# A recommendation tower on one core: eleven one-hot tables instead of ten, three one-hot slots instead of two, and gathers that are waited for by pairs of groups

## The reference

```python
e = jnp.stack([tbl_0[ids[:, 0]], ..., tbl_25[ids[:, 25]]], axis=1)
combined = jnp.concatenate([e, r_dense_x[:, None, :]], axis=1)     # (2048, 27, 128)
interact = jnp.einsum('bfd,bgd->bfg', combined, combined)
z = interact[:, TRIU_I, TRIU_J]                                    # 351 pairs
h = jnp.concatenate([z, r_dense_x], axis=1)
h = jnp.maximum(h @ W_top1 + b_top1, 0.0)                          # 479 x 512
h = jnp.maximum(h @ W_top2 + b_top2, 0.0)                          # 512 x 256
y = h @ W_top3                                                     # 256 x 1
```

## Time and profile before

| | us |
|---|---|
| median of 3 runs (lowest 556.6, highest 562.27) | 556.9 |
| the profiled execution: its time | 551.39 |
| its span, first to last instruction | 549.5 |
| PE busy / DVE / ACT / POOL | 476.3 / 315.8 / 233.9 / 248.9 |
| instructions | 9188 |

### The profile page before, as it was taken

How to read it: one execution, slowest core, us unless ns; L and a number is a source line. 1 busy time by engine, 2 the same in 40 slices (tenths; PEclk the granted TensorE clock), 3 DMA queues, 4 the chain that set the end, 5 groups by cost and what they waited for, 6 DMA issues and landing times.

```text
span 549.5 us, 9188 instructions
## 1 busy us (share of the span) xinstructions
PE 476.3 (87%) x3544; PEld 436.3 (79%) x3544; DVE 315.8 (57%) x503; ACT 233.9 (43%) x755; POOL 248.9 (45%) x266
## 2 busy tenths in 40 slices
PE   3786677998888998899898998989998898899988
PEld 3676576897887888789788888879897887889977
DVE  6994137564467535675366654775367543676252
ACT  3532225443444343534435344443545335354454
POOL 6435554455555554455545445554554545420000
PEclk9998569899899998999999999999999899999999
DMA  8551111111111111111111111111111101100000
GB/s 291 189 151 40 37 38 34 39 39 48 35 39 35 44 39 35 39 38 44 35 35 38 35 49 40 39 35 43 35 40 35 39 24 40 35 21 0 1 2 1
DMA packets 12511, 25.80 MB, mean 47 GB/s; under 512 B 4931, under 2 KB 6603, under 8 KB 12458
## 3 DMA queue, kind: packets, MB, share of 16 engines
q0 software_dynamic: 8192, 16.79, 11.5%
q1 hardware_dynamic: 4276, 8.42, 4.8%
HBM read 25.18 MB, written 0.01 MB: 46 GB/s over the span
## 4 chain that ended last, share of the span: by engine, by line
PE 71%; DVE 10%; DMA 6%; POOL 5%; issue 5%; ACT 2%; another core or an unknown queue 1%; POOLq 0%; DVEq 0%; ACTq 0%
PE x_ps L437 23%; PE gram_ps L453 23%; PE tail_ps L508 13%; DVE onehot L617 8%; DMA raw<-in_tbl,ids_sb 6%; POOL raw L398 4%; PE x_ps L415 4%; PE ids_ps L423 3%; PE tail_ps L478 2%; DVE gram L279 2%; PE tail_ps L487 2%; PE tail_ps L514 2%; DVE split_weights L638 1%; ACT xt L552 0%
## 5 line engine op out<-in xcount | busy, mean ns | idle before, releaser
L398 POOL DMA_INDIRECT raw<-in_tbl,ids_sb x256 | 245.6, 959 | 234.7 <-DMA raw<-in_tbl,ids_sb 161.4
L617 DVE TENSOR_TENSOR onehot<-ids_ps,row_no 128x1024 fp32r<-128x1024 f32 (+1 forms) x160 | 206.7, 1303 | 77.3 <-PE x_ps L437 50.1
L437 PE MATMUL x_ps<-onehot,hot_hi 128*128 128x256 f32 x688 | 185.0, 302 | 24.3 <-DVE onehot L617 17.7
L437 PE MATMUL x_ps<-onehot,hot_lo 128*128 128x256 f32 x688 | 174.4, 286 | 0.0
L437 PEld LDWEIGHTS x_ps<-onehot,hot_hi 128*128 128x128 f32 x688 | 133.3, 194 | 33.2 <-issue 16.4
L453 PE MATMUL gram_ps<-xt 128*128 128x108 f32 x1024 | 137.6, 289 | 14.1 <-DVE gram L279 11.2
L453 PEld LDWEIGHTS gram_ps<-xt 128*128 128x128 f32 x1024 | 129.7, 203 | 21.6 <-ACT gram L279 13.9
L279 DVE COPY gram<-gram_ps 32x104 f32<-32x104 f32 x256 | 68.6, 268 | 117.1 <-PE gram_ps L453 99.7
L437 PEld LDWEIGHTS x_ps<-onehot,hot_lo 128*128 128x128 f32 x688 | 133.6, 194 | 0.0
L279 ACT COPY gram<-gram_ps 32x104 f32<-32x104 f32 x256 | 60.4, 236 | 103.0 <-PE gram_ps L453 73.3
L552 ACT COPY xt<-x_ps 128x256 f32<-128x256 f32 x80 | 49.7, 621 | 99.7 <-PE x_ps L437 91.4
(11 more groups left out here) (48 smaller groups left out, 267.9 us busy)
## 6 DMA issues: line engine op xcount, KB each, us to landing
raw<-in_tbl,ids_sb POOLq DMA_INDIRECT x256, 2.5
table_home<-in_tbl SPq DMA_DIRECT2D x4, 512.0 KB, 8.8
table_home<-in_tbl SPq DMA_DIRECT2D x2, 640.0 KB, 4.2
raw<-in_tbl SPq DMA_DIRECT2D x2, 512.0 KB, 4.7
dense_sb<-in_dense_t SPq DMA_DIRECT2D x8, 128.0 KB
gram<-in_tbl SPq DMA_DIRECT2D x1, 640.0 KB, 12.2
h<-in_tbl SPq DMA_DIRECT2D x1, 512.0 KB, 11.2
h<-in_w SPq DMA_DIRECT2D x1, 256.0 KB
```

What stands on the lines that cost most here:

```text
L398: nc.gpsimd.indirect_dma_start(out=raw[k][:, f, :], out_offset=None, in_=tables[f], in_offset=bass.IndirectOffsetOnAxis(ap=ids_sb[:, t, f: ...
L437: last = nc.tensor.matmul(ps, table[:, chunk_at[j] + c, :], onehot[:, p % RING, c - a, :], start=(c == 0 and table is hot_hi), stop=(c == ...
L617: nc.vector.tensor_tensor(onehot[:, p % RING, 0:n, :], ids_ps[:, it % 2, :].unsqueeze(1).to_broadcast([P, n, BLOCK]), row_no[chunks[it % n ...
```

## The change

- `HOT` 10 to 11: one table of 1250 rows (10 chunks) becomes an item of each block; 15 tables are gathered, in groups of 4, 4, 4 and 3.
- `RING` 2 to 3.
- POOL waits for landed gathers only before groups 0 and 2 of a tile, and there for both of the groups before.
- Room for this in SBUF: `DENSE` 3 to 2; the hot ids are loaded block by block (2 slots, 128 partitions, cleared by POOL first, 11 rows filled by SP) and rounded by DVE block by block; `pick`, 1280 values on 10 partitions, becomes a rounded identity whose column is broadcast as the weights of the ids matmul; `zt` in whole is gone: DVE subtracts `zt_hi` straight from PSUM and gives the bank back; `table_home` reaches over more of the later tiles, so that nine tables load without waiting; the second half of w2 is loaded only after the first part of w1 is split.
- Tail steps are stretched over the 18 pieces of the hot phase and 3 positions more, `TAIL_OVER`, and those past the last piece go between the grams of the first tile.

```diff
-HOT = 10
+HOT = 11
-DENSE = 3
-RING = 2
+DENSE = 2
+RING = 3
-SPREAD = 1.2
+TAIL_OVER = 3
...
-        scale = SPREAD * n / tail_at[-1] if tail_of else 0
+        scale = (n + TAIL_OVER) / tail_at[-1] if tail_of else 0
+        left = [(at * scale, step) for step, at in zip(tail_of, tail_at)]
...
         for i in range(n):
-            steps += [step for step, at in zip(tail_of, tail_at) if i - 1 < at * scale <= i]
+            while left and left[0][0] <= i:
+                steps.append(left.pop(0)[1])
             steps += hot_steps(first + i, first + i + 1)
             steps += [turn for turn, at in zip(turns[0], turn_at) if at == i]
-        steps += [step for step, at in zip(tail_of, tail_at) if at * scale > n - 1]
...
         for i in range(n_gram):
+            while left and left[0][0] <= n + i:
+                steps.append(left.pop(0)[1])
             steps += turns[1][i * n_turn // n_gram:(i + 1) * n_turn // n_gram]
             steps.append(("gram", m + i))
...
             elif kind == "zt":
                 copy(zt_hi[...], src).then_inc(zt_rounded, 1)
-                last = copy(zt[...], src)
+                return
...
+            if kind == "zt":
+                dve.wait_ge(zt_rounded, h * n_kz + j + 1)
+                nc.vector.tensor_tensor(lo, src, hi.bitcast(F32), ALU.subtract).then_inc(zt_split, 1)
+                dve.wait_ge(zt_split, h * n_kz + j + 1)
+                dve.sem_inc(tail_copied[bank], 1)
...
             sp.dma_start(ids_sb[:, :, :], ids).then_inc(ids_in, 16)
-            sp.dma_start(ids_row_in, hot_ids).then_inc(ids_row_landed, 16)
+            sp.wait_ge(ids_raw_cleared, 1)
+            for h in range(2):
+                ids_load(h)
...
-            for k in range(2):
+            for k, landed in ((0, weights_in), (1, rest_weights_in)):
+                if k == 1:
+                    for h in range(1, DENSE):
+                        dense_load(h)
+                    sp.wait_ge(weights_split, 1)
                 sp.dma_start(w2_in[k]..., w2...).then_inc(landed, 16)
             for h in range(blocks):
+                if h + 2 < blocks:
+                    sp.wait_ge(ids_row_ready, h + 1)
+                    ids_load(h + 2)
...
         def _(pool):
+            nc.gpsimd.memset(ids_raw[:, :, :], 0).then_inc(ids_raw_cleared, 1)
             nc.gpsimd.memset(ident[:, :], 0.0).then_inc(consts_ready, 1)
-            nc.gpsimd.memset(pick_in, 0.0).then_inc(consts_ready, 1)
...
                     reach(pool, turn_full[k], (t // RAW - 1) * n_turn + g + 1)
-                    if g > 0:
-                        pool.wait_ge(rows_in[k][g - 1], ...)
-                        pool.wait_ge(last_in[k][g - 1], ...)
-                    elif t > 0:
-                        pool.wait_ge(rows_in[(t - 1) % RAW][n_turn - 1], ...)
-                        pool.wait_ge(last_in[(t - 1) % RAW][n_turn - 1], ...)
+                    if g % 2 == 0 and t + g > 0:
+                        tp, gp = (t, g) if g > 0 else (t - 1, n_turn)
+                        for gl in (gp - 2, gp - 1):
+                            pool.wait_ge(rows_in[tp % RAW][gl], ...)
+                            pool.wait_ge(last_in[tp % RAW][gl], ...)
...
+                pe.wait_ge(ids_row_ready, min(2 * pair + 1, items - 1) // nh + 1)
-                    last = nc.tensor.matmul(ids_ps[:, it % 2, :], pick[:, j, :],
-                                            ids_row[:, h * BLOCK:(h + 1) * BLOCK], start=True, stop=True)
+                    last = nc.tensor.matmul(ids_ps[:, it % 2, :], pick[:, j:j + 1].to_broadcast([P, P]),
+                                            ids_row[:, h % 2, :], start=True, stop=True)
...
-                        for hi, _, src in weight_parts:
+                        for n, (hi, _, src) in enumerate(weight_parts):
+                            if n == len(weight_parts) - 1:
+                                act.wait_ge(rest_weights_in, 16)
                             copy(hi, src).then_inc(weights_rounded, 1)
```

More of the change, by code:

```diff
@@ L176, in build @@
         hot_lo = sb("hot_lo", [P, chunk_at[nh], P], F32R)
-        ids_row = sb("ids_row", [nh, batch], F32R)
-        pick = sb("pick", [nh, nh, P], F32R)
+        ids_raw = sb("ids_raw", [P, 2, BLOCK], I32)
+        ids_row = sb("ids_row", [P, 2, BLOCK], F32R)
+        pick = sb("pick", [P, P], F32R)
         row_no = {n: sb(f"row_no{n}", [P, n]) for n in row_kinds}
@@ L204, in build @@
                 h1[:, :, :].rearrange("p m n -> p (m n)"), gram[:, :, :].rearrange("p q g -> p (q g)")]
-        table, part = 8 * P, 10 * P
-        homes = [(0, 0), (0, table), (1, 0), (1, part), (1, 2 * part), (1, 3 * part), (2, 0), (3, 0), (1, 0), (1, part)][:nh]
+        homes = [(0, 0)] + [(1, 10 * P * n) for n in range(5)] + [(2, 0), (3, 0)] + [(1, 10 * P * n) for n in (5, 0, 1)]
+        homes = homes[:nh]
         hot_in = [flat[b][:, at:at + n * P] for (b, at), n in zip(homes, chunks)]
@@ L216, in build @@
                          for k in range(2)]
-        n_weights = 9
-        ids_row_in = xt[0:nh, :, :].rearrange("j b s -> j (b s)")[:, 0:batch].bitcast(I32)
-        pick_in = xt[0:nh, :, :].rearrange("j b s -> j (b s)")[:, batch:batch + nh * P]
+        n_weights = 8
         x_ps = [psum(f"x_ps{b}", [P, BANK]) for b in range(3)]
@@ L229, in build @@
         hot_landed = [sem(f"hot_landed{j}") for j in range(nh)]
-        ids_row_landed = sem("ids_row_landed")
+        ids_raw_in = [sem(f"ids_raw_in{k}") for k in range(2)]
+        ids_raw_cleared = sem("ids_raw_cleared")
         dense_in = [sem(f"dense_in{k}") for k in range(DENSE)]
         weights_in = sem("weights_in")
+        rest_weights_in = sem("rest_weights_in")
         weights_rounded = sem("weights_rounded")
@@ L308, in tail_copy @@
                 copy(zt_hi[0:kz[j], j, :].rearrange("p (g s) -> p g s", s=QUAD), src).then_inc(zt_rounded, 1)
-                last = copy(zt[0:kz[j], j, :].rearrange("p (g s) -> p g s", s=QUAD), src)
+                return
             elif kind == "h1":
@@ L325, in tail_split @@
             kind, j = key
-            if kind in ("zt", "h1"):
-                bank = tail_bank[key]
+            bank = tail_bank[key]
+            if kind == "zt":
+                dve.wait_ge(zt_rounded, h * n_kz + j + 1)
+                src = tail_ps[bank][0:kz[j], 0:BLOCK].rearrange("p (s g) -> p g s", s=QUAD)
+                hi, lo = (part[0:kz[j], j, :].rearrange("p (g s) -> p g s", s=QUAD) for part in (zt_hi, zt_lo))
+                nc.vector.tensor_tensor(lo, src, hi.bitcast(F32), ALU.subtract).then_inc(zt_split, 1)
+                dve.wait_ge(zt_split, h * n_kz + j + 1)
+                dve.sem_inc(tail_copied[bank], 1)
+            elif kind == "h1":
                 dve.wait_ge(tail_copied[bank], h * tail_per[bank] + tail_nth[key] + 1)
-                rows, whole, hi, lo, split = ((kz[j], zt, zt_hi, zt_lo, zt_split) if kind == "zt" else
-                                              (P, h1, h1_hi, h1_lo, h1_split))
-                nc.vector.tensor_tensor(lo[0:rows, j, :], whole[0:rows, j, :], hi[0:rows, j, :].bitcast(F32),
-                                        ALU.subtract).then_inc(split, 1)
+                nc.vector.tensor_tensor(h1_lo[:, j, :], h1[:, j, :], h1_hi[:, j, :].bitcast(F32),
+                                        ALU.subtract).then_inc(h1_split, 1)
         @block.sync
@@ L620, in make_piece, with ids_round @@
                                         ALU.is_equal).then_inc(piece_ready, 1)
-            dve.wait_ge(ids_row_landed, 16)
-            copy(ids_row[:, :], ids_row_in).then_inc(ids_row_ready, 1)
-            dve.wait_ge(consts_ready, 3 + len(row_kinds))
-            copy(pick[:, :, :].rearrange("j k p -> j (k p)"), pick_in).then_inc(ids_row_ready, 1)
-            dve.wait_ge(ids_row_ready, 2)
+            def ids_round(h):
+                dve.wait_ge(ids_raw_in[h % 2], (h // 2 + 1) * 16)
+                copy(ids_row[:, h % 2, :], ids_raw[:, h % 2, :]).then_inc(ids_row_ready, 1)
+            dve.wait_ge(ids_raw_cleared, 1)
+            ids_round(0)
+            dve.wait_ge(ident_ready, 1)
+            copy(pick[:, :], ident[:, :]).then_inc(pick_ready, 1)
+            dve.wait_ge(consts_ready, 1 + len(row_kinds))
             nc.vector.memset(xt[:, :, feats:], 0.0).then_inc(xt_cleared, 1)
+            rounded = 1
             for (kind, *what), made in zip(order, pieces_made()):
+                if kind == "ids" and rounded <= min(2 * what[0] + 3, items - 1) // nh:
+                    ids_round(rounded)
+                    rounded += 1
                 if kind == "tail":
```

36 lines of the change are left out of this document (15 added, 21 removed).

## The result

The changed kernel takes 613.9 us (604.0 to 618.2, four runs) against 558.5 for the kernel before beside it (556.6 to 562.3): a ratio of 1.099, interval 1.088 to 1.109. Forecast were 547 us and a range of 534 to 564. It is slower by ten per cent.

A forecast was written before the change was run, and what follows sets the result against it. PE was taken to bound blocks 1 to 6, DVE block 0's hot phase. Block 0 -11.1, seven blocks +1.8 and end -0.5 make -9.8 us, applied to the median 556.9: 547 us, range 534 to 564.

The forecast's parts named there:

- Gathers by pairs: POOL's gathers, eight at a time: block 0's first gram phase -16.7 us, its clock -1.5; later blocks gain nothing.
- Eight gathers in flight aren't quicker: Rival, POOL: it waits inside the second four, so block 0's stall stays but for -2.5 us; 563 us, chance 0.08.
- Block 0's stall: PE's waits for gathers in block 0's first gram phase vanish; that phase falls from 27.7 to 11.0 us.
- The eleventh table: Hot phase: +4.4 us on DVE in block 0, +2.66 a block on PE in seven blocks, 18.6.
- Third slot and tail: One-hot ring and tail steps: -2.1 us a block from fewer one-hot waits, -0.3 from steps put between grams.
- Weights: Start of block 0: w2's second half lands late, holding up ACT, DVE and PE's first tail step, +2.0 us.
- The sum but for gathers: Block 0's table +4.4, later table start +0.7, weights +2.0; seven blocks +1.8; end after last block -0.5 us.
- DVE as the bound: Rival, hot phase: DVE's rate sets it, so ring depth doesn't help; some 3.5 us more a block, 570 us, chance 0.07.

The follow-up runs named there:

- the kernel before with plain transfers: Kernel before, POOL starting plain transfers of 128 rows in place of gathers and waiting for them at every second group: 493.8 us.
- gathers 1.9 apart: Changed kernel with a POOL pause (clearing 512 values) ahead of each gather, waiting only for the group two back: 504.2 us, ratio 0.981; again 504.6, ratio 0.908.
- ten tables: Changed kernel with plain transfers of 128 rows in place of gathers, and ten one-hot tables instead of eleven: 478.2 us.
- the kernel of 482 us: Changed kernel with ten one-hot tables, w2's second half in its own place, and a pause (clearing 320 values) ahead of each gather: 482.3 us, ratio 0.871.
- the kernel with gathers in threes: Changed kernel with POOL waiting for landed gathers after every third gather, across groups and tiles: 527.5 us, ratio 0.949; again 526.5, ratio 0.948.
- the short pause: Changed kernel with a pause clearing 8 values ahead of each gather: 503.6 us, ratio 0.976; with ten tables and w2's own place 599.6, ratio 1.084.

## Why the prediction was wrong

**The step that failed** is in "Gathers by pairs": "In later blocks quicker gathers are worth nothing, being off the path". They are off the path as data, and yet their issue reaches PE: eight at a time they hold up its signals, in each gram phase. The kernel with this edit alone lost 55 us, where its terms forecast a gain of 18.2 (-16.7 - 1.5). I had read POOL's rate as if only POOL and PE's turns could feel it. The rows of the kernel before spoke of it already: its gram phases in blocks 1 to 6 took 21.5 to 24.3 us and the last one, with no gathers, 16.2, while PE was idle 6.0 us in each block. Part of that difference is work, since the last phase lacks four pieces: in the kernel before with plain transfers the phases of blocks 1 to 6 take 19.6 us, and PE is idle 1.6 us a block. I laid that idle time to DVE's one-hots and copies, which is what the releaser says, and not to the signal ahead of DVE's copy. What in a gather delays the signal, and why it does so only in some series, stays open. No rival had this step either: "Eight gathers in flight aren't quicker" asks whether POOL slows down, and its spacing stayed 1.25.

**Block 0's stall** went as its mechanism said: no wait of PE for gathers in its first gram phase, first gram at 52.26 against 52.4 forecast. But that phase got late signals in the stall's place: its first 8 grams take 15.6 us at a clock of 0.80 (52.3 to 67.9), against 27.7 before and 11.0 forecast, and the 8 behind them suffer too. From gram phase to gram phase block 0 takes 86.6 us against 84.9, where about -16 were forecast (-16.7 - 1.5 + 2.0). With gathers 1.9 apart it takes 64.7, a gain of 20.2.

**The eleventh table** was nearly right: 23.0 forecast (4.4 + 18.6), 24 to 26 measured. In blocks 1 to 6 it is 3.0 instead of 2.66.

**Third slot and tail** were right together and wrong apart, which is luck. Forecast were -2.1 and -0.3 a block, measured 0.1 and 2.3 us won. The waits for one-hots that the slot was to remove were largely a follow of late signals: without them the kernel before, with its two slots, waits 4.6 us for one-hots at pieces and 4.3 at ids in six blocks, where it had waited 11.4 and 5.5. The gain behind the tail's step is mostly less work on PE, which is busy 323.1 us instead of 334.1 in six blocks: in one block, from start to start, the ids matmuls take 1.4 us in place of 2.1, one-hot matmuls 23.0 in place of 23.6, tail transposes 2.8 in place of 3.5.

**Weights.** PE's first tail step waited 3.27 us in the changed kernel (at 93.14), and 4.76 with gathers 1.9 apart; in the kernel before 2.11. That is +1.2 to +2.6 for a forecast of +2.0. With ten tables PE comes later to that step and waits at ids for DVE instead, 5.64 us with plain transfers and 3.99 in the kernel of 482 us, where w2 has a place of its own.

**The sum but for gathers** was +8.4 (4.4 + 0.7 + 2.0 + 1.8 - 0.5). Measured without late signals: 502.4 or 503.8 less 493.8, +8.6 to +10.0. So the gathers' term made nearly the whole error. The rival on the slower side, DVE as the bound, didn't come: in blocks 1 to 6 DVE is busy 237 of 434 us.

## What to carry to other kernels

Gathers of POOL are not free when nobody waits for them: issued closer than about 1.6 us they delayed PE's own signals here, in the three series of five in which the kernel before took 556 us, by up to 4 us, and PE then ran on at a lower clock. Where an engine stands idle though its producer is done, and two consumers of one signal start at the same moment, look at what POOL issues in that time before blaming the consumer; the releasers "remote" and "issue" often mark the place (in the kernel with gathers in threes, with 11 late signals, "remote" does not appear among the waits). Limit how close gathers follow each other (a pause of 0.4 us ahead of each was enough), not only how many are under way, and measure a change of that rate alone.

## What the runs showed of the hardware that was not expected

- In the 556 series PE's signals arrived 0.5 to 4 us late where each third gather started 2.5 or (on the mean) 2.95 us after the first, and not where it was 3.4; ordinary transfers from POOL's queue, 0.53 us apart, did no such thing. The Trainium skill ("SBUF — State Buffer", SBUF: two separate sides) says of the ports of SBUF that a DMA can't be slowed by a compute operation, "and vice versa". For data that may hold, and no run here tests it; here compute stood still behind gathers, by way of its signals.
- Whether it happens depends on more than the kernel. With gathers 1.47 us apart no signal was late in a 514 series, with 1.48 there were 58 in a 556 series (the latter kernel has ten one-hot tables instead of eleven), and a burst of seven left none late in a 514 series that left them 3.7 us late in a 556 series. One chip gave the kernel before 514 us in one series and 556 in another. The cause stays open.
- After a gather POOL takes 0.30 us before the next, but a memset follows at once (178.18 after 177.23 + 0.95). From its end to the next gather it is 0.27 or 0.52 us, so the short pause costs 0.07 to 0.32 a gather.
- The ids matmul in its new form, on 128 padded partitions and with one column of an identity broadcast as its weights, is the quicker one; which of the two makes it so was not tried. Two of 10 partitions took 0.43 us from start to next start (192.98 to 193.41, the kernel before with plain transfers), two of 128 took 0.34 (189.78 to 190.12, ten tables). I had costed the padding at nothing.
